# Softmax attention as one stream of tiles across batches, with probability copies and routed normalisation on ACT

## The reference, cut to what matters

```
x = x + L0_attn(layernorm(x))
x = x + L0_ffn(layernorm(x))        # routed, 8 experts
q, k, v = h Wq^T, h Wk^T, h Wv^T    # h = layernorm(x), one head of 128
x = x + softmax(q k^T) v / sqrt(128)
x = x + L1_ffn(layernorm(x))        # routed: expert = argmax(layernorm(x) wr + br)
```

## Time and profile before

| | |
|---|---|
| median of 3 runs | 1566.64 us (1566.07 to 1568.64) |
| the profiled execution | 1570.3 us, its span 1568.1 us |
| TensorE, matmuls busy | 1310.5 us, 84% of the span |
| VectorE busy | 1063.9 us, 68% |
| ACT busy | 743.8 us, 47% |
| POOL busy | 694.1 us, 44% |
| first score to start of the last residual | 1107.84 to 1370.76 us |

### The profile page before, as it was taken

How to read it: one execution, slowest core, us unless ns; L and a number is a source line. 1 busy time by engine, 2 the same in 40 slices (tenths; PEclk the granted TensorE clock), 3 DMA queues, 4 the chain that set the end, 5 groups by cost and what they waited for, 6 DMA issues and landing times. The chain is left out here.

```text
span 1568.1 us, 33973 instructions
## 1 busy us (share of the span) xinstructions
PE 1310.5 (84%) x10546; PEld 1014.7 (65%) x10546; DVE 1063.9 (68%) x3597; ACT 743.8 (47%) x1503; POOL 694.1 (44%) x845
## 2 busy tenths in 40 slices
PE   3899999999875999999999964674787887829996
PEld 1566666666644888888888853564555655629996
DVE  3677777777646788888888863565588788722221
ACT  2345454545324676666666632453333333315553
POOL 2344444444320244545353542234366666525665
PEclk9899999999967999999999986998899999959998
DMA  2231212222102000000000004564211111259881
GB/s 79 29 41 26 36 27 33 29 31 31 17 1 81 3 14 8 14 7 14 7 12 9 11 11 123 167 178 118 72 52 46 46 51 45 40 189 312 261 266 40
DMA packets 61575, 100.97 MB, mean 64 GB/s; under 512 B 9698, under 2 KB 36331, under 8 KB 61120
## 3 DMA queue, kind: packets, MB, share of 16 engines
q1 hardware_dynamic: 51648, 78.58, 19.5%
q0 software_dynamic: 9856, 21.52, 4.4%
HBM read 62.96 MB, written 29.75 MB: 59 GB/s over the span
## 5 line engine op out<-in xcount | busy, mean ns | idle before, releaser
L1137 DVE TENSOR_TENSOR m_Sl<-m_S,m_Sh 128x512 fp32r<-128x512 f32 x256 | 174.8, 692 | 32.5 <-ACT m_S L1049 27.6
L1049 ACT ACTIVATE m_S<-PS,W 128x512 f32<-128x512 f32 x256 | 175.6, 686 | 33.4 <-PE PS L957 30.2
L1403 POOL DMA_INDIRECT rows<-r_row,r_posi x128 | 143.0, 1117 | 35.6 <-issue 35.6
L1389 POOL TENSOR_TENSOR r_soft<-r_euler,r_soft 128x32 f32<-128x32 f32 x16 | 86.9, 5429 | 132.5 <-DVE r_soft L1287 132.5
L1044 ACT ACTIVATE m_Sh<-PS,W 128x512 fp32r<-128x512 f32 x128 | 88.2, 689 | 106.2 <-PE PS L957 105.0
L750 DVE TENSOR_TENSOR am<-PS,C 128x512 f32<-128x512 f32 x192 | 119.4, 677 | 19.9 <-PE PS L442 19.9
L955 PE MATMUL PS<-m_HH,m_w1h 128*128 128x512 f32 x256 | 110.7, 432 | 14.5 <-DVE m_HL L1101 14.3
L1608 PEld LDWEIGHTS PS<-f_wt,f_hid 128*128 128x128 f32 x960 | 119.5, 192 | 4.2
L1608 PE MATMUL PS<-f_wt,f_hid 128*128 128x128 f32 x960 | 119.9, 275 | 0.0
L1597 PE MATMUL PS<-f_xT,f_wt 128*128 128x256 f32 x480 | 119.9, 387 | 0.0
L343 POOL TENSOR_TENSOR am<-am,C 128x512 f32<-128x512 f32 x64 | 81.4, 1272 | 80.2 <-ACT am L623 80.2
(11 more groups left out here) (242 smaller groups left out, 3242.5 us busy)
## 6 DMA issues: line engine op xcount, KB each, us to landing
f_wt<-wr SPq DMA_DIRECT2D x40, 578.0 KB
f_row<-rows SPq DMA_DIRECT2D x40, 260.0 KB
f_wt<-wr SPq DMA_DIRECT2D x40, 256.0 KB, 2.8
f_row<-rows SPq DMA_DIRECT2D x40, 132.0 KB, 2.1
mid<-f_res SPq DMA_DIRECT2D x40, 128.0 KB, 2.6
rows<-r_padding SPq DMA_DIRECT2D x16, 260.0 KB
X<-x SPq DMA_DIRECT2D x16, 256.0 KB, 5.5
qr<-qphi SPq DMA_DIRECT2D x64, 64.0 KB
```

Of the source, the lines that this page charges most:

```text
L1049: nc.scalar.activation(S[:, n % 3, :], PS[:, n % 3, :], ACT.Silu, bias=w("b1")[:, n:n + 1]).then_inc(s_ready, 1)
L1137: nc.vector.tensor_tensor(Sl[:, n % 4, :], S[:, n % 3, :], Sh[:, n % 4, :].bitcast(F32), ALU.subtract).then_inc(sl_ready, 1)
L1403: nc.gpsimd.indirect_dma_start(out=self.rows, out_offset=bass.IndirectOffsetOnAxis(ap=self.posi[:, u, t:t + 1], axis=0), in_=self.row[:, u ...
```

## The change

`stages` is replaced by `over_steps`, in which every engine runs step(b) for b from -3 to 18, the middle ones (4 to 13) in a loop of two. A step walks over the four tiles of batch b. At tile t TensorE issues the score of that tile, the transposes of the tile before it and the weighing of the tile two before it; for t = 0 and 1 these belong to the batch before. The front of b+1 and the routing of b-2 (count, place and scatter: of b-3) stand at fixed tiles in each step. Weighing goes to bank 6 or 1, by the parity of the batch; y and the values share bank 0 with the transposed xn, so the values now wait for the copy of y.

The copies of the transposed probabilities move from VectorE to ACT. So does the routed normalisation with the ids: VectorE computes one shift (-mean times inverse deviation, `dve_shift`), ACT applies it. The factor 1/sqrt(128) goes into the weights w("v1") in `setup`, and the scaling of the inverse goes. The row sums get two buffers. The gather runs one batch further ahead (b+3), and `pool_begin` stands before the first one.

The core of the diff, with the four steps in the order POOL, TensorE, ACT, VectorE; `tile(b, t, lag)` gives the batch and tile that lie `lag` tiles back, and `exists(b)` is true for the 16 batches:

```diff
-            nc.vector.tensor_scalar(w("o"), w("o"), 0.5, None, ALU.mult).then_inc(made, 1)
+            nc.vector.tensor_scalar(w("o"), w("o"), 0.5, None, ALU.mult)
+            nc.vector.tensor_scalar(w("v1"), w("v1"), float(P) ** -0.5, None, ALU.mult).then_inc(made, 1)
...
+    def dve_shift(self, dve, b, u, turn):
+        dve.wait_ge(self.rstd_ready, b + 1)
+        after_previous(dve, self.xn_ready, b)
+        self.nc.vector.scalar_tensor_tensor(self.shift[:, :], self.mv[:, :, 0], -1.0, self.rstd[:, :], ALU.mult,
+                                            ALU.mult).then_inc(self.shift_ready, 1)
...
+    def act_normalise(self, act, b, u, turn):
+        act.wait_ge(self.shift_ready, b + 1)
+        if not isinstance(turn, int) or turn:
+            act.wait_ge(self.scattered[u], 16 * CT * turn)
+        nc.scalar.activation(self.row[:, u, :, COL_ID:COL_ID + 1], self.c("ids")[:, bass.ds(b * CT, CT)].unsqueeze(2), ACT.Copy)
+        for t in range(CT):
+            xt = self.X[:, bass.ds(b * CT + t, 1), :].rearrange("p o d -> p (o d)")
+            ins = nc.scalar.activation(self.row[:, u, t, 0:P], xt, ACT.Identity, bias=self.shift[:, t:t + 1],
+                                       scale=self.rstd[:, t:t + 1])
+        ins.then_inc(self.xn_ready, 1)
...
+        def over_steps(eng, step):
+            for b in range(STEPS[0], LOOP[0]):
+                step(b, b % 2, (b - 2) // 2)
+            with eng.Fori(0, (LOOP[1] - LOOP[0]) // 2) as i:
+                for u in range(2):
+                    step(i * 2 + (LOOP[0] + u), (LOOP[0] + u) % 2, i + 1)
+            for b in range(LOOP[1], STEPS[1]):
+                step(b, b % 2, (b - 2) // 2)
...
+            def step(b, u, turn):
+                ending = isinstance(b, int) and b == BATCHES
+                if exists(b + 3):
+                    fetch(b + 3, 1 - u)
+                if ending:
+                    routing.pool_inverse_deviation(pool, b + (-1), 1 - u, None)
+                if exists(b + (-3)):
+                    routing.pool_scatter(pool, b + (-3), 1 - u, None)
+                if exists(b + 2):
+                    inverse_deviation(b + 2)
+                if exists(b + (-1)) and not ending:
+                    routing.pool_inverse_deviation(pool, b + (-1), 1 - u, None)
...
+            def values(b, u):
+                pe.wait_ge(y_ready, b + 1)
...
+            def step(b, u, turn):
+                for t in range(CT):
+                    if exists(b):
+                        score(b, u, t)
+                    lagging = tile(b, t, 1)
+                    if lagging:
+                        attend(*lagging)
+                    if t == 1 and exists(b + 1):
+                        turn_xn(b + 1)
+                    if t == 2 and exists(b + (-2)):
+                        routing.pe_turn(pe, b + (-2), u, None)
+                    if t == 3 and exists(b + (-2)):
+                        routing.pe_scores(pe, b + (-2), u, None)
+                    lagging = tile(b, t, 2)
+                    if lagging:
+                        weigh(lagging[0], u if t >= 2 else 1 - u, lagging[1])
+                    if t == 0 and exists(b + (-3)):
+                        routing.pe_count(pe, b + (-3), 1 - u, None)
+                    if t == 2 and exists(b + 1):
+                        project(b + 1, 1 - u)
+                    if t == 3 and exists(b + 1):
+                        values(b + 1, 1 - u)
...
+            def step(b, u, turn):
+                for t in range(CT):
+                    lagging = tile(b, t, 1)
+                    if lagging:
+                        copy_p(*lagging)
+                    if exists(b):
+                        exps(b, u, t)
+                    if t == 0 and exists(b + (-2)):
+                        routing.act_normalise(act, b + (-2), u, turn)
+                    if t == 1 and exists(b + 1):
+                        copy_x(b + 1, 1 - u)
+                    if t == 2 and exists(b + (-2)):
+                        routing.act_copy_xT(act, b + (-2), u, None)
+                    if t == 2 and exists(b + 1):
+                        copy_y(b + 1, 1 - u)
+                    if t == 3 and exists(b + (-2)):
+                        routing.act_copy_x(act, b + (-2), u, None)
+                    if t == 3 and exists(b + 1):
+                        copy_v(b + 1, 1 - u)
...
+            def step(b, u, turn):
+                for t in range(CT):
+                    if exists(b):
+                        largest(b, t)
+                    if t == 0 and exists(b + 1):
+                        normalise(b + 1)
+                    if t == 0 and exists(b + (-2)):
+                        routing.dve_shift(dve, b + (-2), u, None)
+                    if t == 1 and exists(b + (-1)):
+                        residual(b + (-1), 1 - u)
+                    if t == 1 and exists(b + (-3)):
+                        routing.dve_place(dve, b + (-3), 1 - u, None)
+                    if t == 2 and exists(b + 2):
+                        stats(b + 2, u)
+                    if t == 3 and exists(b + (-1)):
+                        routing.dve_statistics(dve, b + (-1), 1 - u, None)
+                    if t == 3 and exists(b + (-2)):
+                        routing.dve_pick(dve, b + (-2), u, None)
```

More of the change, by code:

```diff
@@ L1790, in softmax_attention, with exists, tile, not_first @@
                           bank=7, scattered=scattered, x_ready=x_ready)
[L1792 to L1801, removed]
-                for u in range(2):
[L1803 to L1811, removed]
+        OUT = (6, 1)
+        LOOP = (4, 14)
+        STEPS = (-3, BATCHES + 3)
+        def over_steps(eng, step):
+            for b in range(STEPS[0], LOOP[0]):
+                step(b, b % 2, (b - 2) // 2)
+            with eng.Fori(0, (LOOP[1] - LOOP[0]) // 2) as i:
+                for u in range(2):
+                    step(i * 2 + (LOOP[0] + u), (LOOP[0] + u) % 2, i + 1)
+            for b in range(LOOP[1], STEPS[1]):
+                step(b, b % 2, (b - 2) // 2)
+        def exists(b):
+            return not isinstance(b, int) or 0 <= b < BATCHES
+        def tile(b, t, lag):
+            b, t = (b, t - lag) if t >= lag else (b + (-1), t - lag + CT)
+            return (b, t) if exists(b) else None
+        def not_first(b, t, n):
+            return not isinstance(b, int) or CT * b + t >= n
         @block.sync
@@ L1837, in fetch @@
                         in_offset=bass.IndirectOffsetOnAxis(ap=where_now[:, u, t:t + 1], axis=0)).then_inc(fetched[u], 16)
[L1839 to L1847, removed]
+            def step(b, u, turn):
[10 more added lines that the diff above has]
+                    routing.pool_inverse_deviation(pool, b + (-1), 1 - u, None)
             routing.pool_begin(pool)
[L1849 removed]
+            over_steps(pool, step)
             routing.pool_end(pool)
[L1851 removed]
         @block.tensor
@@ L1876, in a @@
-            def a(b, u, nxt, sent):
-                def score(t):
-                    pe.wait_ge(y_ready, b + 1)
[L1879 to L1930, removed]
@@ L1931, in _, with turn_xn, project @@
-            stages(pe, f, a, steps(pe, routing.pe_turn, routing.pe_scores, routing.pe_count))
+            def turn_xn(b):
+                pe.wait_ge(xn_ready, b + 1)
+                after_previous(pe, v_ready, b)
+                for t in range(CT):
+                    mm = nc.tensor.transpose(PS[:, 0, t * P:(t + 1) * P], xn[:, t, :], ident)
+                mm.then_inc(xT_psum, 1)
+            def project(b, u):
+                pe.wait_ge(xT_ready, b + 1)
+                pe.wait_ge(qk_ready, 1)
+                nc.tensor.matmul(PS[:, 0, :], qk[:, :], xT[:, u, :], start=True, stop=True).then_inc(y_psum, 1)
@@ new lines, in attend, with weigh @@
+            def attend(b, t):
+                pe.wait_ge(prob_ready, CT * b + t + 1)
+                if not_first(b, t, 2):
+                    pe.wait_ge(pT_ready, CT * b + (t - 1))
+                for m in range(CT):
+                    mm = nc.tensor.transpose(PS[:, 4 + t % 2, m * P:(m + 1) * P], prob[:, t % 2, m * P:(m + 1) * P], ident)
+                mm.then_inc(pT_psum, 1)
+            def weigh(b, u, t):
+                pe.wait_ge(pT_ready, CT * b + t + 1)
+                if t == 0:
+                    pe.wait_ge(v_ready, b + 1)
+                    if not_first(b, 0, 2 * CT):
+                        pe.wait_ge(x_ready, b + (-1))
+                for m in range(CT):
+                    mm = nc.tensor.matmul(PS[:, OUT[u], t * P:(t + 1) * P], probT[:, t % 2, m * P:(m + 1) * P], v[:, u, m, :],
+                                          start=(m == 0), stop=(m == CT - 1))
+                mm.then_inc(out_psum, 1)
@@ L1933, in _ @@
+            over_steps(pe, step)
         @block.scalar
@@ L2058, in _ @@
             routing.dve_begin(dve)
-            stages(dve, f, a, steps(dve, routing.dve_statistics, routing.dve_normalise, routing.dve_pick, routing.dve_place))
```

(1 more changed line is left out.)

212 lines of the change are left out of this document (81 added, 131 removed).

## The result

The changed kernel takes **1526.5 us** (median of 4 runs, 1523.3 to 1529.4) against 1567.6 (4 runs, 1566.1 to 1569.0) of the kernel before beside it: ratio 0.974, 95% interval 0.972 to 0.976. Forecast were 1522 and a range of 1512 to 1540. The profiled execution took 1526.6, where the sum made against its counterpart said 1526.0.

A forecast was written before the change was run, and what follows sets the result against it. No engine was full; TensorE waited some 4.2 of 16.97 us per batch at the seam between batches. Twelve steps of 13.65 plus start and end gave 50.0 less, 5.7 lost, net 44.3: 1522 us, range 1512 to 1540.

The forecast's parts named there:

- The terms and the loop: TensorE's queue in the softmax attention: 12.7 us of matmuls per batch, 13.65 with waits, twelve steps 163.8.
- The wait of about 1 us at pe_turn: TensorE, each routed batch: pe_turn waits for place behind the residual and last weighing, going at 7.39 instead of 6.4.
- Just fits: POOL's fetch, scatter and two deviations take 13.43 us per batch, busy 98% of the time.
- POOL becomes the bound: Rival: gathers stretched by VectorE make the period 14.1 to 15.0, time 1528 to 1539; POOL or small waits 0.17.
- pool_begin moves ahead of the first fetch, and nothing follows from it: Section start: the move costs nothing, since both stood before the first deviation; first score at 1108.9 instead of 1107.84.
- attend 0 at 2.62: First step: tile 0's transposes come 2.62 us after its score's start, as on an undisturbed tile.
- the first step: First batch step of the section, from the first score: 10.0 us.
- Second and third: Next two batch steps: 11.3 us, complete but for routing, and 12.6 with pe_turn and router scores.
- The end: Batch 15's normalisation waits for batch 13's scatter; padding starts 20.8 us after the residual instead of 15.1, 5.7 lost.
- The sum: Last residual at 1320.8 against 1370.76, 50.0 us less; 5.7 lost at the end, net 44.3 gained.
- fewer things stand ahead of a maximum: VectorE: up to 4.2 us of work leaves it per batch; the gain is the shorter queue, not that time.
- the stream does not run: Rival: ACT's order or seams add a wait per batch, period about 15.2, time 1541; chance 0.13.

The follow-up runs named there:

- place_first: Changed kernel with VectorE's place of batch b-3 put before the residual of b-1 instead of behind it; 1517.1 us, ratio to before 0.969.
- cheap_deviation: Changed kernel with POOL's power in the second layer's deviations made a multiplication (values change); 1523.4 us, single execution.
- begin_late: Changed kernel with pool_begin, which releases SP's padding, after the first two fetches instead of before them; 1527.0 us, single execution.
- after_again: The changed kernel, unedited, run again as control beside variants on another chip; 1526.4 us.
- third_row: Changed kernel with a third buffer of rows and positions for batch 15; 1551.8 us, single execution.
- all_three: Changed kernel with place before the residual, pool_begin after the first fetches and a third row buffer for batch 15; 1512.8 us, ratio 0.965.
- before_copies_on_act: Kernel before the change, with only its copies of the probabilities moved to ACT; 1569.0 us, ratio 0.999.
- norm_on_vector: Changed kernel with the routed normalisation back on VectorE; 1546.5 us, and 1525.6 when repeated on another chip.

## Why the prediction was right

**The terms and the loop: right.** The twelve loop steps took 165.6 us, 13.80 each, where 13.65 was forecast (163.8). The wait of about 1 us at pe_turn is there, it ends with VectorE's place, and place_first removed it. 0.05 of the 0.15 is the loop itself (13.70 in cheap_deviation and begin_late). The other 0.10 is VectorE's CAST at the end of place, which stands in that loop. Two rows of POOL and VectorE in the change:

```profile
1190.39 0.94 POOL L1865 DMA_INDIRECT s_G<-mid,s_where_now  x1 [0.30 <-issue]
1190.91 0.42 DVE L1338 CAST r_posi<-r_pos 128x4 int32<-128x4 f32 x1
```

The CAST ends at 1191.33, with POOL's issue, instead of after its usual 0.17, and the period that it stands in is 13.95 instead of 13.70. Eight of the twelve CASTs do so, with 0.25 to 0.42 us, and by as much as each is stretched its period is longer than 13.70, to about 0.01 us. In after_again it is four of them (mean period 13.75); in begin_late and cheap_deviation no CAST is stretched and no period in the loop is above 13.71. Which batches are hit depends on how far into one of POOL's issues the CAST begins: 0.52 us or more in the eight, 0.34 in one of the change that was not stretched, up to 0.51 in after_again.

**POOL: the stretch was sized right, its coupling named right.** "Just fits" was 13.43; between its copies after place_first it is 13.4. The rival *POOL becomes the bound* happened in small. The ten issues of a scatter in the change that began while VectorE's sum of the gathered rows (L2020) ran took 1.01 to 1.45 us: 0.88 to 0.92 us and the time of the overlap. The Trainium skill (SBUF — State Buffer, Who interferes with whom) says that a VectorE instruction with two inputs in SBUF contends with a GpSimd instruction that reads SBUF. The trace agrees: L2020 adds two tiles in SBUF, and the scatter reads its positions there. It also says that where a VectorE instruction in a two-port mode, as a cast can be, contends with GpSimd, the one issued first blocks the other; the stretched CASTs, which end with POOL's issue, agree, though no run shows in which mode they ran.

**The start: wrong in the step "pool_begin moves ahead of the first fetch, and nothing follows from it".** What follows is that SP's padding transfers are let go ahead of the first gathers, which then land after 5.7 us (4.7 to 5.7 in ten runs) instead of 2.7. The first score came 2.0 later in the section, not 1.1 (1.4 in after_again, and 0.9 to 1.3 in the six runs in which the landing took 5.0 or less). A second term was too small: "attend 0 at 2.62" was read from a start at full clock, though the sum had the values just before it at half. In the change the granted clock is 0.50 from 1107.5 to 1111.5, the first two scores run in it, and attend 0 stands at 3.5. So the first step took 11.0 instead of 10.0. Second and third, 10.95 and 12.6, were forecast as 11.3 and 12.6.

**The end: right.** Padding starts 20.6 after the residual, forecast 20.8 against 15.1; third_row (17.3) and all_three (14.3, against 20.0 of place_first) show that it is the wait for the scatter of batch 13.

**The sum.** 50.0 were forecast to the residual, 46.2 came: 0.9 lost at the start, 0.7 in the first three steps together, 1.8 in the loop, 0.3 in the last batch (14.5 for 14.2). 5.5 instead of 5.7 went at the end. That gives 40.7 for the section, and 2.6 came from outside it, as between any two executions: 43.3 of span, 44.3 forecast. The profiled agreement to 0.6 us is therefore partly luck; the medians say 41.1.

**What the sum could not say.** The prediction listed the work that leaves VectorE, up to 4.2 us a batch, ahead of the order, and wrote that "fewer things stand ahead of a maximum". The runs rank them otherwise: the copies alone in the old order bring nothing, and with either transfer alone taken back the new structure keeps all but some 1 us of its 41. So nearly the whole gain lies in that structure: the order, with transposes a tile late and weighings two, across batches, and what came with it, a second bank for the weighings and the gather a batch further ahead. Both transfers taken back together was not run, and the parts of the structure were not run apart.

**Left open.** What made the clock fall on one chip is not settled: a chip, a moment, or an execution whose batches lie otherwise. The old order kept its clock there (before_copies_on_act: 1.00 and a period of 16.85). The prediction's rival *the stream does not run* gave 1541 for a further wait of 1.5 us a batch; norm_on_vector's 1546.5 has such a size, with another cause.

## What to carry to other kernels

Put what an in-order engine needs least urgently last: the change's place stood behind a residual that waits for the newest weighing, and swapping the two was worth 9 us. Before moving work between engines ask whether a seam stands in the queue: here a lighter VectorE gained nothing while it stood, and once it was gone the move was hardly needed. And run the unedited version beside its variants, on the same chip: three kernels here looked 20 to 35 us bad for a reason that wasn't in them.

## What the runs showed of the hardware

A kernel of fp32 matmuls whose TensorE waits 1 us of each 13.7 kept the full clock through its loop on two chips. On a third, three variants of it lost the clock again and again; for the two that were run again elsewhere this cost 21 and 31 us. From 1150 to 1210 us each fall of the granted clock in these three stands behind idle time in TensorE's rows, of 1 to 3 us at a stretch, and is over after a few microseconds.

Near these falls TensorE's rows can't be trusted to the microsecond. Three rows of third_row, of TensorE and ACT:

```profile
1253.24 1.14 PE L1938 MATMUL PS<-s_v,s_probT 128*128 128x128 f32 x8
```

```profile
1253.07 0.60 ACT L1980 ACTIVATE s_yT<-PS 128x512 f32<-128x512 f32 x1 [2.37 <-remote]
1253.80 0.60 ACT L1995 ACTIVATE s_probT<-PS 128x512 f32<-128x512 f32 x1
```

The weighing is shown 1.2 us before the end of the copy that it reads, and the copy of y, whose projection stands at 1250.27, 1.7 us late with the releaser "remote". By this TensorE ended its work later there than its rows say; that it ran slower than the granted clock of its rows is likely and not shown. From 1110 to 1360 us 43 waits of VectorE and ACT in those three kernels name "remote", with up to 5.1 us each, and none in any other run.

Small instructions of VectorE and the issues of POOL's indirect DMAs hold each other up: a CAST of 128x4 ended with the issue beside it (0.25 to 0.42 us instead of 0.17), and an issue that began beside VectorE's sum of two tiles in SBUF took 0.88 to 0.92 us and the overlap. And eight padding transfers of SP just ahead of a gather made its landing 4.7 to 5.7 us instead of 2.6 to 2.7.
